# Two MLP stages: where VectorE adds the second layer's results, and when GpSimd adds bias and residual

## The reference

```
# block 0 (after a Fourier mixing that gives xs; residual is x)
xm  = layernorm(xs) * norm2_w + norm2_b
out = xs + residual + gelu(xm @ mlp_w1 + mlp_b1) @ mlp_w2 + mlp_b2
# block 1 (x is the block's input plus the result of a gated scan of 8 steps)
xn2 = layernorm(x) * norm2_scale + norm2_bias
out = x + gelu_tanh(xn2 @ mlp_w1 + mlp_b1) @ mlp_w2 + mlp_b2
```

## Time and profile before

| what | us |
|---|---|
| median of three runs (lowest, highest) | 1177.94 (1177.81, 1183.68) |
| the profiled execution, its device time | 1178.18 |
| the span of its instructions | 1176.4 |
| first MLP, from the first transpose to the last group's second layer | 307.6 to 557.5 and on |
| second MLP, the same | 927.6 to 1166.3 and on |
| busy over the span: TensorE, VectorE, ScalarE, GpSimd | 1073.1, 802.3, 726.2, 347.3 |

### The profile page before, as it was taken

One profiled execution on the slowest core, in us unless ns is written; L12 is line 12 of the kernel. 1 busy time (PEld: TensorE's weight loads), 2 busy tenths in 40 slices (PEclk: granted clock), 3 DMA queues, 4 the chain that ended last, 5 costly groups with the idle time before them and its releaser, 6 DMA issues. The chain is left out here.

```text
span 1176.4 us, 25740 instructions
## 1 busy us (share of the span) xinstructions
PE 1073.1 (91%) x9160; PEld 824.8 (70%) x9160; DVE 802.3 (68%) x2102; ACT 726.2 (62%) x1325; POOL 347.3 (30%) x373
## 2 busy tenths in 40 slices
PE   2659999997899999999799999999999699999998
PEld 1349988885588888888555655655654488888887
DVE  4746465553578877776688699699699567666665
ACT  2647565554666677666676567566635266766665
POOL 1260111122222222221337347258158211111110
PEclk9879999898899999999899999999999699999999
DMA  6888799767400000000100000000000000000001
GB/s 133 282 204 178 146 179 177 149 124 202 136 1 0 0 0 0 0 0 0 48 1 1 1 1 1 1 1 1 1 1 1 1 14 27 27 27 27 27 27 41
DMA packets 140217, 64.21 MB, mean 55 GB/s; under 512 B 115824, under 2 KB 134928, under 8 KB 140128
## 3 DMA queue, kind: packets, MB, share of 16 engines
q1 hardware_dynamic: 133176, 38.31, 15.8%
q0 software_dynamic: 5248, 17.68, 5.6%
q10 hardware_dynamic: 1712, 7.11, 1.9%
HBM read 44.21 MB, written 12.58 MB: 48 GB/s over the span
## 5 line engine op out<-in xcount | busy, mean ns | idle before, releaser
L1086 PE MATMUL L_conv_ps<-w2hl,L_conv_hhi 128*128 128x384 f32 x768 | 228.1, 365 | 7.8 <-DVE X L986 7.2
L902 ACT ACTIVATE L_conv_hf<-L_conv_ps,L_conv_b 128x512 f32<-128x512 f32 x192 | 131.9, 687 | 150.5 <-PE L_conv_ps L1067 142.2
L976 DVE TENSOR_TENSOR L_conv_hlo<-L_conv_hf,L_conv_hhi 128x512 fp32r<-128x512 f32 x192 | 139.5, 741 | 104.6 <-ACT L_conv_hhi L911 101.9
L1086 PE MATMUL L_conv_ps<-w2hl,L_conv_hlo 128*128 128x192 f32 x768 | 188.3, 252 | 0.0
L855 POOL TENSOR_TENSOR X<-X,L_conv_b 128x192 f32 x128 | 72.5, 598 | 358.0 <-DVE L_conv_xn L961 358.0
L1201 POOL TENSOR_TENSOR sc_lo<-XS,sc_hi 128x512 fp32r<-128x512 f32 x96 | 142.4, 1498 | 114.4 <-ACT sc_hi L1277 114.4
L1086 PEld LDWEIGHTS L_conv_ps<-w2hl,L_conv_hhi 128*128 128x128 f32 x768 | 144.2, 188 | 13.7 <-DVE L_conv_hlo L976 7.2
L1086 PEld LDWEIGHTS L_conv_ps<-w2hl,L_conv_hlo 128*128 128x128 f32 x768 | 146.2, 191 | 0.0
L1277 ACT ACTIVATE sc_hi<-XS 128x512 fp32r<-128x512 f32 x144 | 87.6, 629 | 81.9 <-DVE XS L1342 27.6
L634 PE MATMUL psF<-spectrum,X 100*24 100x64 f32 x4352 | 128.3, 290 | 7.7 <-issue 5.0
L634 PEld LDWEIGHTS psF<-spectrum,X 100*24 100x24 f32 x4352 | 121.4, 121 | 17.0 <-issue 16.4
(11 more groups left out here) (150 smaller groups left out, 2143.3 us busy)
## 6 DMA issues: line engine op xcount, KB each, us to landing
X<-in_L_conv_w SPq DMA_DIRECT2D x136, 144.0 KB
XS<-in_x POOLq DMA_DIRECT2D x8, 768.0 KB, 6.6
rows_spectrum<-XS POOLq DMA_DIRECT2D x8, 768.0 KB, 4.3
d<-rows_spectrum ACTq DMA_DIRECT2D x8, 768.0 KB, 5.0
X<-in_x SPq DMA_DIRECT2D x8, 768.0 KB, 9.6
out<-X SPq DMA_DIRECT2D x15, 384.0 KB, 2.6
XS<-d POOLq DMA_DIRECT2D x48, 96.0 KB, 4.4
spectrum<-in_L_conv_mlp_w SPq DMA_DIRECT2D x2, 576.0 KB, 6.8
```

The costliest lines, as they stand in the source:

```text
L902: nc.scalar.activation(hf[:, m % 3, :], ps[:, RB + m % 2, :], gelu, bias=b1[:, m:m + 1]).then_inc(act1, 1)
L976: nc.vector.tensor_tensor(hlo[:, m, :], hf[:, m % 3, :], hhi[:, m, :].bitcast(F32), ALU.subtract).then_inc(h_lo, 1)
L1086: mm = pe.matmul(o, x, w, start=(m == 0 and n == 0), stop=(m == MT - 1 and n == 1), skip_group_check=True)
```

## The change

GpSimd's group 0 still waits for `normalise(0)`; every later group i waits for `h_lo` at 6 i, which VectorE reaches with the last `low_hidden` of group i-1. GpSimd's loop over the groups is now `rolled` (the first group apart, the others in a loop). In VectorE's group i two outputs of group i-1 come ahead of `normalise(i+1)`, the third behind it and ahead of the first `low_hidden`, the fourth between the first and the second `low_hidden`. The arithmetic is the same, and both MLPs are changed, since they are one function.

```diff
             def group(i):
-                pool.wait_ge(normed, GT * (i + 1))
+
+                if isinstance(i, int) and i == 0:
+                    pool.wait_ge(normed, GT)
+                else:
+                    pool.wait_ge(h_lo, MT * i)
                 for k in range(GT):
                     nc.gpsimd.tensor_tensor(X[:, GT * i + k, :], X[:, GT * i + k, :], b2[:, :],
                                             ALU.add).then_inc(biased if XS is None else based, 1)
...
-            with pool.Fori(0, N) as i:
-                group(i)
+            rolled(pool, N, group, 1, 0)
...
                 low_channels(i)
+                if not head:
+                    output(i - 1, 0)
+                    output(i - 1, 1)
                 if not (isinstance(i, int) and i == N - 1):
                     normalise(i + 1)
+                if not head:
+                    output(i - 1, 2)
                 for m in range(MT):
-                    if not head and m < GT:
-                        output(i - 1, m)
                     low_hidden(i, m)
+                    if not head and m == 0:
+                        output(i - 1, 3)
```

## The result

The changed kernel is faster: median 1165.97 us of 4 runs (1163.35 to 1166.54) beside 1177.88 (1177.04 to 1183.68) of the kernel before on the same chip, ratio 0.9886 [0.986, 0.9912]. Its profiled execution took 1166.52, with a span of 1164.6.

The account below looks back on a forecast made before the run. A loop through VectorE bounds the first MLP (3.80 + 5.70 + 6.56 = 16.06 us), TensorE almost alone the second. Savings of 7.6 and 2.0 sum to 9.6 from 1178.18: 1168.6, or 1168.4 against the median; range 1164.8 to 1173.2.

Parts of the forecast that it names:

- six source periods: First MLP, groups 1 to 6, with source statistics: transposes to next group's transposes, forecast at 15.47 us each.
- six periods behind the table loads: First MLP, groups without source statistics after ScalarE's table loads: 14.80 us each plus an allowance of 0.3, saving 2.55.
- period with the table loads: First MLP, the 16.91 us period with ScalarE's table loads, which start when its last high part is made: -1.06.
- last stretch: End of the first MLP, 541.51 to 557.46, with a wait for the outputs: 15.95 to 14.85 us, -1.10.
- Low parts are free, E comes 1.06 earlier: First MLP: without GpSimd's additions, VectorE's last low part ends 2.74 us after the group's transposes, not 3.80.
- rival (c): Chance 0.03: all VectorE statistics take turns with GpSimd's five additions; source periods 18.8, others 16.7, about 1200 us.
- The copies pay: VectorE's small copies to mv wait for GpSimd: L1005 loses about 0.25 us, L954 waits out the long addition.
- Then the split starts at E + 4.70 and TensorE goes at E + 6.17: Source-statistics groups: first-layer input split and TensorE's restart, timed from the last low part's end; period 15.47 us.
- Without source statistics, go at E + 5.56 behind a split that waits for the long addition: First MLP: TensorE resumes 5.56 us after the last low part, once the second input split ends; period 14.80.
- Rival (a): Chance 0.18: neither small copy waits and no addition holds the first split long; periods 15.11 and 14.70, -13, 1165 us.
- Rival (b): Chance 0.16: GpSimd's long addition precedes the first split in every group, copy L954 pays in full; -4.3, 1173.6 us.
- Rival (d): Additions still reach into the next group's low parts, as before; given nothing beyond Rival (b).

## Why the prediction came out as it did

The mechanism is the one forecast, and the sizes were too small: the two stages gained 13.6 us where 9.6 were predicted. Three terms of the sum failed, and they hold 3.8 of the missing 4.0 us: the six source periods (15.47 forecast, 15.24 measured on average; 2.9 us forecast, 4.3 measured), the six periods behind the table loads (14.80 forecast, 14.68 measured; 2.55 and 3.6) and the second MLP (2.0 and 3.35). By its steps, with before's terms as the prediction has them:

| term | predicted | measured |
|---|---|---|
| first MLP: first two periods | -0.6 | -1.2 |
| four source periods of 16.05 | -2.3 | -3.1 |
| period with the table loads | -1.06 | -1.08 |
| six periods without source statistics | -2.55 | -3.6 |
| last stretch | -1.1 | -1.2 |
| second MLP | -2.0 | -3.35 |

- *Low parts are free, E comes 1.06 earlier.* Right: E lies 2.72 behind the transposes, the longest low part is 695 ns, and the table-load period, which hangs on E through ScalarE, moved by 1.08. The kernel before without the long addition and the run with GpSimd's wait alone show that this is the cause.
- *bn_stats and bn_aggr pay nothing.* Right: over the whole first MLP, shortest, median and longest are in the changed kernel

```profile
L998 DVE BATCH_NORM_STATS2 L_conv_st<-X x64: 351/355/360, 341.6 to 557.5; 128x6 f32 x52, 128x6 f32<-128x192 f32 x12
L1006 DVE BATCH_NORM_AGGREGATE L_conv_mvb<-L_conv_st x64: 147/149/181, 342.8 to 558.3; 128x2 f32<-128x6 f32 x64
```

  and 352/355/361 and 147/151/182 in the kernel before, although they now lie under the bias additions; rival (c) falls.
- *The copies pay.* Right in kind, for L957. The Trainium skill (SBUF — State Buffer, Who interferes with whom) counts tensor_scalar among the operations that can enter a 2-port mode and then contend with GpSimd. The trace agrees, for 8 values a partition: 0.81 with the long addition beside it, 0.17 with that left out.
- *Then the split starts at E + 4.70 and TensorE goes at E + 6.17.* This step failed, in its size. The split started at 391.59 - 387.15 = E + 4.44, and the go was E + 5.89, 0.28 less. With 2.72 ahead of it and 6.62 behind it that makes the period of 15.23 shown above, where 15.47 was predicted. I had the copy end at E + 4.65 and the split start 0.05 behind that. The copy ended at E + 4.53, 0.03 behind the addition and not 0.10, and the split started 0.09 ahead of its recorded end. The 0.34 of issue that stands ahead of the split in the earlier trace rows ran under the hold. Of the 0.64 us by which the copy is longer, 0.22 reach the split (0.72 from start to start against 0.50). And L1008 lost 0.07, not 0.25.
- *Without source statistics, go at E + 5.56 behind a split that waits for the long addition.* The wait is there as forecast (2.22), but the splits ended at 468.92 = E + 5.28 (E is 462.35 + 1.29 = 463.64), before TensorE's own work was through at E + 5.44. I had L864 start at E + 3.10, behind the first split; it started at E + 2.65. So these periods are TensorE alone and not, as predicted, 0.12 above it. And the 0.3 that I allowed for the second reciprocal was not needed: its period took 14.70, the others 14.65 to 14.72.
- *What TensorE alone takes, and the second MLP.* This step failed too. I put TensorE's period at 14.68, called 15 of these, 220.2, the floor of the second MLP, and took 2.0 of the 3.4 us down to it. The stage reached 220.27. That the floor fits is in part luck: the periods of the changed kernel are 14.57 to 14.64, and the one with the table loads, which the floor left out, is 15.81; the two errors cancel. Where the 3.35 us lay shows from the start of a group's transposes to the start of its second layer, before and after:

```profile
986.89 1.03 PE L1051 MATMUL L_conv_ps<-ident,L_conv_xn 128*128 128x128 f32 x8
987.80 0.43 PE L1086 MATMUL L_conv_ps<-w2hl,L_conv_hhi 128*128 128x384 f32 x1
```

```profile
978.31 1.03 PE L1059 MATMUL L_conv_ps<-ident,L_conv_xn 128*128 128x128 f32 x8
979.10 0.43 PE L1094 MATMUL L_conv_ps<-w2hl,L_conv_hhi 128*128 128x384 f32 x1
```

  It is 0.91 and 0.79 here; over the fourteen groups it is 0.79 to 0.97 before and 0.78 or 0.79 after, 1.2 us in sum, and no wait is marked there. The last stretch gave another 1.06, of which 0.62 stood as a wait. The second layers are 0.8 shorter in sum (6.92 to 7.04 each before, 6.91 to 7.01 after), the first layers 0.3; what makes one of them longer than another is not shown. The run with VectorE's order alone has 221.2 there, the one with GpSimd's wait alone 223.8 (before: 223.6, and 224.0 without the long addition), so the gain is the order's, up to the scatter of 0.6 between traces.
- *Outputs ahead of the normalisation cost nothing.* Right: no wait of TensorE for xn shows in the changed kernel save for the first group of each MLP, as before.

Rival (a)'s time, 1165, is the nearest of all, with periods of 15.11 and 14.70, but for another reason: not that the copies are free, but that most of their wait lies over time that was lost anyway. (By the predicted periods free copies are worth 6 x 0.36 = 2.2 us, and not the 2.5 named.) Rival (b) did not happen: without source statistics the first split issued ahead of L864 (465.88 against 466.29), and with them the split came at E + 4.44 and not at E + 5.0. Rival (d) did not happen: the additions end 2.8 us ahead of the normalisation (391.65 to 394.49).

```profile
394.49 1.25 DVE L964 TENSOR_SCALAR L_conv_xn<-XS,mv,L_conv_rs 128x192 f32 x4
```

## What to carry to other kernels

Where two engines exclude each other for the length of an instruction, ask on which chain the loser's queue lies: the same addition of 1.85 us cost the first MLP 9.6 us where it met the low parts and 2.1 where it meets the statistics and the splits. A hold is not added to what follows it: the issue of the next instruction goes on below it, so take the later of both ends and not their sum. And read an engine's floor from a stretch in which its waits are shown to be gone: gaps of about 0.1 us in most groups of the second MLP, 1.2 us in all, stood in no list of waits.

## What was not expected of the hardware

A tensor_scalar copy of 8 values a partition was held for the rest of a GpSimd addition (0.81 against 0.17 us), as a larger one of the scan was before (1379 ns against a median of 332). bn_stats of X ran at 0.36 us beside GpSimd's additions to X. And when VectorE's normalisation and a low part meet a row of GpSimd additions, both sides pay: four normalisations 2.12 us for 1.25, a low part 1.00 for 0.69, the four bias additions 2.39 for 2.28.
